# Macaron block (NVFP4 feed-forward, attention, feed-forward): a root by Newton steps on VectorE, the turn of the maxima ahead of the gather, and x loaded ahead of the codes

## What is computed

```python
x = h                                        # [1, 2048, 256] float32
x = x + 0.5 * ffn(layernorm(x), Wg, Wu, Wd)  # 256 -> 2048 -> 256, gelu(gate) * up
x = x + attn(layernorm(x), Wq, Wk, Wv, Wo)   # 16 heads of 16, causal softmax
x = x + 0.5 * ffn(layernorm(x), Wg, Wu, Wd)
```

## Time and profile before

| what | value |
|---|---|
| time, median of 3 runs | 1143.03 us (1140.59 to 1145.18) |
| the profiled execution's own time | 1144.71 us |
| its span | 1142.6 us |
| TensorE busy | 1084.0 us (95%) |
| VectorE busy | 691.7 us (61%) |
| ScalarE busy | 583.8 us (51%) |
| first gate/up product | at 20.5 us |
| attention | 349.9 to 841.8 us |

### The profile page before, as it was taken

How to read it: one execution, slowest core, us unless ns; L and a number is a source line. 1 busy time by engine, 2 the same in 40 slices (tenths; PEclk the granted TensorE clock), 3 DMA queues, 4 the chain that set the end, 5 groups by cost and what they waited for, 6 DMA issues and landing times. The chain is left out here.

```text
span 1142.6 us, 17555 instructions
## 1 busy us (share of the span) xinstructions
PE 1084.0 (95%) x6448; PEld 708.7 (62%) x6448; DVE 691.7 (61%) x1595; ACT 583.8 (51%) x1115; POOL 111.5 (10%) x409
## 2 busy tenths in 40 slices
PE   4999999998998888899999999999989999999998
PEld 3888888886875333333333333333257888888887
DVE  5986545448374556788888888888333434344333
ACT  5764443433336545666776777677752423324222
POOL 1000000000001226222111111111100000000000
PEclk9999999999998878999999999999999999999999
DMA  6001030250121711332022202200000000000000
GB/s 190 2 24 24 10 120 1 47 149 1 44 88 27 201 33 34 77 60 51 2 52 52 46 7 52 52 2 1 1 1 1 1 11 10 1 19 1 19 1 19
DMA packets 75222, 43.80 MB, mean 38 GB/s; under 512 B 47161, under 2 KB 68993, under 8 KB 75137
## 3 DMA queue, kind: packets, MB, share of 16 engines
q1 hardware_dynamic: 75137, 42.68, 15.3%
HBM read 25.63 MB, written 16.78 MB: 37 GB/s over the span
## 5 line engine op out<-in xcount | busy, mean ns | idle before, releaser
L984 ACT ACTIVATE attn_prob<-psum 128x512 f32<-128x512 f32 (+3 forms) x640 | 299.3, 541 | 145.6 <-PE psum L669 144.7
L1124 DVE TENSOR_REDUCE attn_part_max<-psum 128x1 f32<-128x512 f32 x384 | 243.0, 685 | 58.9 <-PE psum L684 57.2
L581 PE MATMUL psum<-ffn_xt,all_w_hi 128*128 128x512 f32 x512 | 167.0, 407 | 0.0
L1320 PE MATMUL psum<-ffn_xt,all_w_hi 128*128 128x512 f32 x512 | 162.2, 398 | 2.4 <-DVE ffn_xt L1457 2.4
L728 PE MATMUL psum<-attn_prob,attn_vals 128*32 128x512 f32 (+3 forms) x1280 | 160.6, 555 | 2.2 <-POOL attn_prob L503 1.2
L1127 DVE CUSTOM_DVE_ANT_0 attn_junk<-psum,attn_mask 128x128 bf16<-128x128 f32 (+3 forms) x256 | 117.1, 486 | 30.3 <-PE psum L684 30.0
L1467 DVE TENSOR_TENSOR ffn_act_out<-ffn_act_out,psum 128x512 f32<-128x512 f32 x64 | 44.0, 688 | 112.1 <-ACT ffn_act_out L1390 111.8
L1320 PEld LDWEIGHTS psum<-ffn_xt,all_w_hi 128*128 128x128 f32 x512 | 92.4, 189 | 20.5 <-DVE ffn_xt L1457 2.6
L1390 ACT ACTIVATE ffn_act_out<-psum 128x512 f32<-128x512 f32 x64 | 38.3, 599 | 129.6 <-PE psum L1320 129.6
L581 PEld LDWEIGHTS psum<-ffn_xt,all_w_hi 128*128 128x128 f32 x512 | 92.0, 190 | 17.5
L596 PE MATMUL psum<-all_w_hi,ffn_inner 128*128 128x256 f32 x512 | 102.2, 283 | 0.1
(11 more groups left out here) (131 smaller groups left out, 1535.6 us busy)
## 6 DMA issues: line engine op xcount, KB each, us to landing
qk_rows<-qkv_parts SPq DMA_DIRECT2D x16, 384.0 KB, 2.6
qk_rows<-qkv_parts SPq DMA_DIRECT2D x16, 256.0 KB, 3.0
attn_q_early<-qk_rows SPq DMA_DIRECT2D x8, 384.0 KB, 4.2
attn_q_late<-qk_rows SPq DMA_DIRECT2D x8, 384.0 KB, 3.7
attn_k_mid<-qk_rows SPq DMA_DIRECT2D x3, 768.0 KB, 7.0
attn_k_late<-qk_rows SPq DMA_DIRECT2D x3, 768.0 KB, 6.9
all_x<-in_L_attn_h SPq DMA_DIRECT2D x4, 512.0 KB, 6.3
v_rows<-qkv_rows_v SPq DMA_DIRECT2D x16, 128.0 KB, 2.6
```

Of the source, the lines that this page charges most:

```text
L581: last = nc.tensor.matmul(psum[:, 2 * m + q % 2, :], w_part[a][:, 3 * g + m, pl, o:o + P], xt[:, b % 2, c, pl, :], start=(n == 0), stop=(n ...
L984: nc.scalar.activation(prob[:, n % PRING, at:BT], psum[:, S0 + n % SBANKS, at:BT], ACT.Exp).then_inc(s["exp"], 1)
L1124: nc.vector.tensor_reduce(to, psum[:, bank, :], AX.X, ALU.max).then_inc(s["max_read"], 1)
L1320: last = nc.tensor.matmul(psum[:, 2 * m + q % 2, :], w_part[a][:, 3 * g + m, pl, o:o + P], xt[:, b % 2, c, pl, :], start=(n == 0), stop=(n ...
```

## The change

Seven edits. (1) The root of block 3's norm for the projections is computed on VectorE, by a shift, a scale, a subtraction from a constant and three Newton steps of three instructions: twelve instructions of 128x4, each but the second waiting for the one before it. ScalarE's square root there is gone, and with it the two loads of activation tables around it. (2) The turn of the maxima stands after tile j = 0 of its step on TensorE, ahead of a gather in the same step, and ScalarE's copy after the exp of that tile; the numbering of the shared bank follows. (3) The turn of group 3 moves from step 0 to step 1. SP's list keeps its order. (4) x of block 0 is loaded ahead of the codes of job 0. (5) ScalarE does `weight_high(0)` ahead of `split(0)`. (6) VectorE does `weight_low(0)` ahead of `split(0)`. (7) A semaphore and a small tile are added for the root.

```diff
+        newton = sb("newton", [P, 3, SUB], F32)
+        def inverse_root(dve, s, use, b):
+            tiles = slice(b * SUB, (b + 1) * SUB)
+            v, y, half, t = var_eps[:, tiles], newton[:, 0, :], newton[:, 1, :], newton[:, 2, :]
+            n = ROOT_OPS * use
+            nc.vector.tensor_scalar(t.bitcast(I32), v.bitcast(I32), 1, None, ALU.logical_shift_right).then_inc(s["newton"], 1)
+            nc.vector.tensor_scalar(half, v, -0.5, None, ALU.mult).then_inc(s["newton"], 1)
+            dve.wait_ge(s["newton"], n + 2)
+            nc.vector.tensor_scalar(y.bitcast(I32), t.bitcast(I32), -1.0, MAGIC, ALU.mult, ALU.add).then_inc(s["newton"], 1)
+            for step in range(3):
+                dve.wait_ge(s["newton"], n + 3 * step + 3)
+                nc.vector.tensor_tensor(t, y, half, ALU.mult).then_inc(s["newton"], 1)
+                dve.wait_ge(s["newton"], n + 3 * step + 4)
+                nc.vector.tensor_tensor(t, t, y, ALU.mult).then_inc(s["newton"], 1)
+                dve.wait_ge(s["newton"], n + 3 * step + 5)
+                if step < 2:
+                    nc.vector.scalar_tensor_tensor(y, t, 1.5, y, ALU.add, ALU.mult).then_inc(s["newton"], 1)
+                else:
+                    nc.vector.scalar_tensor_tensor(rstd[:, tiles], t, 1.5, y, ALU.add, ALU.mult).then_inc(s["rstd"], 1)
...
-            turn_at = [-2, -2, -2, 0] + [chunk_at[ends[g]] + 2 for g in range(EARLY, NG_A)]
+            turn_at = [-2, -2, -2, 1] + [chunk_at[ends[g]] + 2 for g in range(EARLY, NG_A)]
...
                 for d in range(-2, NS):
+                    for g in turned(d):
+                        turns[g] = n
+                        n += 1
                     if gathered(d) is not None:
                         gathers[gathered(d)] = n
-                        n += 1
-                    for g in turned(d):
-                        turns[g] = n
                         n += 1
...
                         load_scales(0)
+                        load_x(0)
                         load_codes(0)
-                        load_x(0)
...
                             for g in turned(d):
-                                max_row(g)
+                                if g >= EARLY:
+                                    max_row(g)
...
                                 for e, hd in maxima_behind(d, j):
                                     maxima(2 * e + hd)
+                                if j == 0:
+                                    for g in turned(d):
+                                        if g == EARLY - 1:
+                                            pe.wait_ge(s["added"], NB)
+                                        turn_max(g)
...
                                 if j == 2 and gathered(d) is not None:
                                     gather(gathered(d))
-                            for g in turned(d):
-                                if g == EARLY - 1:
-                                    pe.wait_ge(s["added"], NB)
-                                turn_max(g)
...
                         root(0)
+                        weight_high(0)
                         split(0)
-                        for n in range(2):
-                            weight_high(n)
+                        weight_high(1)
...
+                                if j == 0:
+                                    for t in turned(d):
+                                        copy_max(t)
...
-                            for t in turned(d):
-                                copy_max(t)
-                            if d == 0:
-                                root(Q_USE[NB - 1])
...
-                            dve.wait_ge(s["std"], use + 1)
-                            nc.vector.reciprocal(rstd[:, tiles], deviation[:, tiles]).then_inc(s["rstd"], 1)
+                            if use == Q_USE[NB - 1]:
+                                dve.wait_ge(s["var"], use + 1)
+                                inverse_root(dve, s, 0, b)
+                            else:
+                                dve.wait_ge(s["std"], use + 1)
+                                nc.vector.reciprocal(rstd[:, tiles], deviation[:, tiles]).then_inc(s["rstd"], 1)
...
                         decode(1)
+                        weight_low(0)
                         split(0)
                         scale_weight(1)
-                        weight_low(0)
                         weight_low(1)
```

More of the change, by code:

```diff
@@ L94, in norm_stats @@
             return last
+        ROOT_OPS = 11
+        MAGIC = float(0x5F3759DF)
+        def inverse_root(dve, s, use, b):
[16 more added lines that the diff above has]
+                    nc.vector.scalar_tensor_tensor(rstd[:, tiles], t, 1.5, y, ALU.add, ALU.mult).then_inc(s["rstd"], 1)
         def turn_tensor(xb, bank):
@@ L1511, in build_program @@
         F1_SEMS = NORM + "stats xt_turned gu product inner_lo down added xt_hi xt_lo gelu inner_hi x0 x1 x2 x3 "
-        Q_SEMS = ("loaded loaded_o wt wfull wt_hi wt_lo unit v_sum v bias_q full part_1 part_2 part_3 rest "
+        Q_SEMS = ("newton loaded loaded_o wt wfull wt_hi wt_lo unit v_sum v bias_q full part_1 part_2 part_3 rest "
                   "part_out0 part_out1 v_out0 v_out1 v_out2 v_out3 ")
```

## The result

| | before | after |
|---|---|---|
| time, median of 6 runs each | 1143.22 us (1140.59 to 1145.77) | 1139.05 us (1136.27 to 1139.34) |
| ratio, 95% interval | | 0.9953 (0.994 to 0.9966) |
| the profiled execution: own time, span | 1144.71, 1142.6 | 1138.86, 1137.2 |
| mean granted clock over the span | 0.980 | 0.983 |
| TensorE busy | 1084.0 us | 1082.1 us |

Faster by 4.2 us, a third of the 13.1 forecast. The interval of the ratio excludes 1, though the prediction had put its own bar for "faster" at 5.7 us.

What follows compares the result with a forecast made beforehand. TensorE's waits and its clock early in the attention were taken to bound the kernel; 1.15 + 1.45 - 4.8 - 2.7 - 8.2 = -13.1 us against 1144.71 gave 1131.6, say 1132 us, with a range of 1128 to 1141.

Steps and rivals of the forecast that it cites:

- bar for "faster": Whole kernel: about 0.5%, 5.7 us, is what a measurement can tell from no change; faster means under 1137.3 us.
- What bounds the kernel: TensorE is busy nearly everywhere; its waits count, and its clock, which falls only in slices 12 to 15.
- The start: Kernel start: loading x ahead of the codes and two reorderings delay TensorE's first product, +1.15 us.
- The root: Norm of block 3: twelve Newton-step instructions take 2.37 us against 0.92, all on the path, +1.45 us.
- The table loads: Norm of block 3: removing two table loads gives nothing, since they lie beside TensorE's wait for VectorE.
- rival (c): Norm of block 3: table loads were on the path, removal gains 2 x 1.28 us, total 1127.6 us; chance 0.06.
- The turn: Attention: the earlier turn of the maxima removes waits for their rows, -4.8 us, and for `normalise`, -2.7 us.
- The clock: 400 to 445 us: with the waits gone, the half-clock stretches probably go too, -8.2 us.
- (a): Attention: the clock stays low and only the direct waits go, 1139.8 us; chance 0.28.
- (b): Attention: the turn becomes the wait, 28 turns at 0.5 us each, +14 us, 1153.8 us; chance 0.04.
- (d): Steps 11 to 48: saved waits return as waits for VectorE's reads of the maxima banks, 1147.3 us; chance 0.06.
- signs to look for: New profile: later first turn, twelve VectorE instructions, 4.6 us idle, no table load, two waits gone, 400-420 us clock above 0.9.

Runs made afterwards that it cites:

- E10: E5 with the new start (x ahead of the codes, parts of job 0 ahead of the splits): 1128.5 us.
- E9: E5 with the root of block 3 by Newton steps on VectorE: 1126.03 us.
- E1: The kernel after, with GpSimd's masks of a step ahead of the splits of the maxima: 1128.87 us, ratio 0.9883.
- E2: The kernel before with only the moved turns of the maxima (edits 2 and 3), plus the unused semaphore and tile: 1133.82 us, ratio 0.9924.
- E3: The kernel after, with the root of block 3 on ScalarE again instead of Newton steps: 1135.21 us.
- E4: The kernel after, with the old start (codes of job 0 ahead of x, its parts behind the splits): 1137.25 us.
- E5: E2 with GpSimd's masks ahead of the splits, root and start as before: 1127.57 us, ratio 0.9864.
- E11: The kernel of E5 measured again, as base for E9 and E10: 1126.31 us, ratio 0.9849.
- E6: The kernel before, with GpSimd's masks ahead of the splits and nothing else: 1140.6 us, ratio 0.9967.
- E7: The kernel before, with only x loaded ahead of the codes of job 0; one run: first turn of job 2's codes 0.54 us later.
- E8: The kernel before, with only job 0's high and low parts ahead of the splits; one run: first turn of job 2's codes at 20.49 us.

## Why the prediction was wrong, step by step

**What bounds the kernel**: right in its places, TensorE's waits and the clock of slices 12 to 15. The step did not weigh in `weigh`'s own 2.2 us of waits in the stretch, at 454 and 516 us.

**The start, +1.15**: +1.04 at the first turn, from two halves, 0.54 and 0.57, where it had 0.5 and 0.75. The mechanism was right; that the sum fits so well is partly luck, as the turn moves by some 1.4 us on average over the executions. By E10 step 12 moves by 1.6 and the median by 0.9 to 2.2.

**The root, +1.45**: the idle time grew by 1.38 (0.20 us for each instruction, as worked out), but by E9 only some 0.7 of it reaches step 12, because part of the idleness fell into stretches at half clock. That none is lost on the way, "all on the path", was too simple. **The table loads, nothing**: right; ScalarE idles for 5.92 us there, and rival (c) falls. By the Trainium skill's 2.66 us for a switch ("ScalarE: Activation LUTs", What ACT_TABLE_LOAD costs) the two switches gone would be, as an estimate, 5.3 us; no run shows a gain from them, and the row says why: ScalarE is not what the next work waits for.

**The turn, -4.8 and -2.7**: both groups went, 5.0 and 3.2 us. The sum of TensorE's waits from 376 to 520 us went from 17.3 to 10.4 us, by 6.9, near the 7.5. But as the next thing to be late the step named only the gather, at 0.5 us. It was `weigh`, whose waits went from 2.2 to 4.1 us. It also set the turn itself at nothing. From 526 us on, where hardly anything waits, the stretch with 15 turns is 2.0 us longer in every kernel with the moved turn (306.6 to 308.6 in the table), 0.13 us a turn. Before, the turn shared its start with `weigh` (the timeline of before, and of after, one step):

```profile
616.51 1.07 PE L728 MATMUL psum<-attn_prob,attn_vals 128*32 128x512 f32 x8
...
619.18 0.23 PE L691 MATMUL psum<-all_identb,attn_max_parts 128*24 128x128 bf16 x1
619.20 1.07 PE L728 MATMUL psum<-attn_prob,attn_vals 128*32 128x512 f32 x8
```
```profile
612.79 1.06 PE L753 MATMUL psum<-attn_prob,attn_vals 128*32 128x512 f32 x8
...
614.17 0.23 PE L716 MATMUL psum<-all_identb,attn_max_parts 128*24 128x128 bf16 x1
...
615.58 1.06 PE L753 MATMUL psum<-attn_prob,attn_vals 128*32 128x512 f32 x8
```

From `weigh` to `weigh` it was 2.69 us, and is 2.79. The steps without a turn in this stretch take 2.79 us on average in both kernels.

**The clock, -8.2: this is the step that failed.** "If the waits are gone, so, probably, are these stretches" took the waits named to be the only ones that could bring the clock down. The time at 1.2 GHz fell by 7.0 us (45.7 to 38.7), not by 24: at 0.39 that is 2.7 us in place of 8.2. Waits of `weigh`, of 1.22, 0.78 and 1.06 us, shorter than the two that the step named, stood right ahead of the half clock at 408, 431 and 510 us, and a further stretch appeared at 268 us. With the masks first (E1) the two stretches that the step counted are gone, and the time at 1.2 GHz is 20.9 us less than before.

The price of 0.39 was right. In E1 steps 12 and 13 run at the full clock: from 402.43 to 408.48 us, less 0.34 of waits, they take 5.71 us of work, where the kernel before had 9.40 at half clock, and 3.69 of 9.40 is 0.39. At that price 20.9 us are worth 8.2, as forecast, in a kernel without the second kind of wait.

The terms as measured or estimated, 1.04 + 0.7 - 6.9 - 2.7 + 2.0 for the turns' place, give -5.9. Two more belong to it: 2.0 off in the second feed-forward (last section) and, as an estimate, 13 x 0.13 = 1.7 on for the attention's earlier turns. That makes -6.2, against spans that differ by 5.4. Of the 7.7 us between forecast and spans the clock is 5.5.

**The rivals.** The value is that of (a), 1139.8, but its cause isn't: E1 has the full clock where (a) said that other things than waits keep it down. What (a) was built on was a misreading, too. TensorE did wait between 409 and 419 us, for 1.15 us ahead of the score at 412.98, which stands in the earlier trace rows. (b) charged the turn with 0.5 us; it was 0.13, and by TensorE's own pace, not by GpSimd's parts. (d) named VectorE for waits that come back; it was GpSimd. Of the signs to look for, 21.3 us, the twelve instructions, 4.6 us, the absent table loads and the two absent waits came; the clock over 0.9 did not, and that was the sign that decided. At 0.83 it was not under the 0.7 either that the prediction had named as its refutation, so its own signs left the case open.

## What to carry to other kernels

When a wait on the path is taken away, walk through each other engine's list in the same steps for work that stands behind a wait of its own and has a reader: here eight masks behind one split whose result nobody wanted for two steps. The move of the turn with that one reordering and nothing else of the change gives 1126 to 1128 us, 1.4 to 1.5% under before, and no kernel here is clearly faster. And before you price a gain in clock, list every wait in the stretch, not the longest alone: here waits of 0.78 to 1.22 us that remained were followed by half clock as well.

## What was not expected of the hardware

**The same wait is followed by half clock in one execution and not in another.** Four kernels have the moved turn and all four waits at `weigh` (after, E2, E3, E4). The first wait, of 1.21 or 1.22 us, has a stretch at half clock right behind it in all four. The second, of 0.72 to 0.78, has one in after and E4 but not in E2 and E3; the third, of 1.02 to 1.06, in E4 alone; the fourth, of 1.04 to 1.06, in after and E4, and not in E2, E3 or the kernel before. A wait of 2.73 us for VectorE's maxima at about 268 us (2.71 before) has one behind it in after and none in before. It isn't the code that decides this: E5 and E11 are one kernel, both have the wait of 2.73 us, and only E11 has the half clock behind it. Windows of E5 and then of E11:

```profile
262.00:280.00 18.00, 13.81 (x73) 1.00 0.00 1
```
```profile
262.00:280.00 18.00, 14.84 (x72) 0.91 0.00 1
```

With the waits at `weigh` and at the rows of the maxima both gone, no trace (E1, E5, E9, E10, E11) has half clock between 392 and 820 us, and the mean clock of all 21 runs is 0.988 to 0.991, against 0.982 to 0.991 in the 25 runs with the waits at `weigh`. So taking the waits away is shown to work; what decides whether one that stays is followed by half clock no run here shows.

The second feed-forward, whose code no kernel changed, is some 2 us shorter wherever the turn was moved: the first and last down products (L1336) of before start at 874.7 and 1139.0 us, those of after (L1365) at 871.1 and 1133.5, 264.3 against 262.4 us, at full clock and without a wait. E1 to E5 and E9 to E11 all have 262.4, E6, E7 and E8 264.3 or 264.4. The gate and up products take 389 to 392 ns on average in place of 395, the down products 283 in place of 280. It happens to cancel the 2.0 us of the turns. The kernels with the moved turn also all carry the added semaphore and tile of edit 7, and the others don't, so the runs don't tell which of the two it goes with. Its cause stays open.
